# Index tables of a graph kernel: the counts by source come first, VectorE picks places beside the target one-hots, and the sync engine stores the fetched target rows

## The chip, the cores and the metric

The kernel runs on one core of a Trainium2 chip. The metric is the device time of one execution, in microseconds. Each execution runs the whole program: 73632 instructions in the profiled one.

## The reference

The program computes four graph networks one after the other over N = 50000 nodes and E = 25000 edges (`src`, `dst`) with rows of D = 128 floats: a two-layer graph attention, three hops of weighted sums, one round of edge messages, and three layers of a graph convolution, each behind a layer norm with a residual sum. What matters here is the shape that all of them share:

```python
h = gat_conv(x, src, dst, edge_attr, ...)            # gathers rows by src, sums them by dst
msgs = edge_val[:, None] * x[edge_col]               # edge_col = dst: gathers by dst ...
segment_sum(msgs, edge_row, num_segments=n)          # ... sums by edge_row = src
```

So rows are fetched by source and summed by target, or the other way round. The kernel needs for each node the position of its edges in an order by target (the edges come sorted so) and in an order by source, which it makes itself. For that it builds a table `TAB` with two numbers per node, and for each edge a place (`sort_place`) in the first pass of a sort by source. The stage in question makes these two things and copies, beside them, the row `x[dst]` of each edge into a DRAM array `XD`.

## The kernel before, in words

The program is a row of stages, each a block in which all engines take part, and a stage begins when the one before it has ended on every engine. Semaphores order the work inside a stage; nothing in it is placed by a planner.

The 25000 edges lie as 128 partitions by T = 196 columns, and a column is worked on as one tile. Columns go in NB = 14 blocks of U = 14. A node number is split into a low digit (0 to 255, R = 256) and a high digit; one-hot rows of 256 elements for the two digits, multiplied by TensorE, count nodes into a 256 by 256 histogram in PSUM.

`phase_tables` (L533) is the stage that changes. Its engines do this:

- VectorE makes the one-hots of the **source** digits, two instructions a column (L597, L598), into a ring of two blocks. Before block k it waits until TensorE has used block k - 2 (`s_freed`).
- ScalarE makes the one-hots of the **target** digits: two instructions a column (L652, L653) and, at the end of a block, two wide ones (L658) over the whole block. Its ring has two blocks too, and `d_freed` frees them.
- TensorE takes block k of the source (3 matmuls a column, 42 in all, L668 and L669), then block k of the target (2 a column, 28 in all, L675), then block k + 1 of the source, and so on in strict turn. After the last block it signals `counted`.
- VectorE then copies the four count tiles, scans them, has TensorE add over partitions (L682, L685 to L687), forms the table (L622 to L635), signals `tabled`, forms `weights`, and runs `pick_places` (L520): 196 instructions, one a column, of growing length 256 to 451, L525.
- The sync engine waits for `tabled` and writes `TAB`.
- GpSimd runs `fetch_target_rows` (L498): 14 gathers of 128 rows a block into a ring of two blocks (`xd_ring`, L511), and after block k it waits for the gathers of block k - 1 and stores them to `XD` (L504, 896 KB). Before block k it waits for the store of block k - 2, and, by `beside` (L489), for `d_freed` to reach k - 2.

The next stage, `phase_front`, reads `TAB` by 392 gathers on GpSimd from its first instruction on (L473). A later stage, `phase_high_digit` (L693), runs the same `pick_places` while GpSimd gathers.

## Time and profile before

| what | us |
|---|---|
| runs shown, median | 6715.88 |
| runs shown, lowest and highest | 6671.08, 6734.13 |
| profiled execution, first to last instruction | 6034.3 |
| median less this span | 681.6 |
| stage of the tables, POOL's first row to the next stage's first | 141.57 to 508.29 |

The page has no time of the profiled execution itself, only its span; what lies around the span is known as the difference of 681.6 us to the median. The table's last line gives the start of the first index instruction of the stage and of the first DMA issue of the next one. Busy shares of the whole span say little about this stage, which is one of a dozen: VectorE is busy 68% of the span, GpSimd 62%, TensorE 55%, ScalarE 48%. The page's chain of work that ended last is empty here (0% on each engine), so what ends a wait is read from the waits and the timeline of the stage.

### The profile page before, as it was taken

How to read it: one execution, taken by the hardware profiler on the slowest of the kernel's cores; microseconds unless marked ns; L12 is line 12 of the kernel's file. 1: busy time of each engine (PE TensorE's matmuls, PEld its weight loads, DVE VectorE, ACT ScalarE, POOL GpSimd, SP SyncE). 2: the span in 40 equal slices, each digit the busy share in tenths (PEclk: the TensorE clock that was granted, in tenths of full speed). 3: DMA queues.
4: the chain of work that ended last, by engine and by line, in shares of the span. 5: the costliest groups of instructions: out<-in, count | busy, mean ns of one | idle time of the engine just before them, and what ended most of it. 6: DMA issues, size and time to landing. Idle time of an engine off the chain costs nothing. (4 is left out here: it accounts for less than half of the span.)

```text
span 6034.3 us, 73632 instructions
## 1 busy us (share of the span) xinstructions
PE 3347.4 (55%) x17186; PEld 2352.5 (39%) x17363; DVE 4133.5 (68%) x14902; ACT 2890.5 (48%) x6936; POOL 3733.6 (62%) x3700
## 2 busy tenths in 40 slices
PE   0534777737330000777777758888688854454443
PEld 0423554627320000444444436666466644343322
DVE  7359999639491995998989967777377755454332
ACT  0954777313100222666666647777477743232110
POOL 0664776767675576645536546665577627676776
PEclk9767999767665555899999989999899976566666
DMA  2223665637321664434435445554244447564333
GB/s 67 80 93 119 199 200 189 191 91 192 84 51 43 163 186 124 121 109 110 116 100 121 110 128 186 189 188 158 84 151 150 141 143 246 175 200 145 119 123 100
DMA packets 512359, 827.25 MB, mean 137 GB/s; under 512 B 108999, under 2 KB 193843, under 8 KB 510796
## 3 DMA queue, kind: packets, MB, share of 16 engines
q1 hardware_dynamic: 396011, 629.55, 32.2%
q0 software_dynamic: 115936, 193.21, 14.3%
q8 instruction: 136, 2.23, 0.2%
q14 instruction: 276, 2.26, 0.1%
HBM read 382.25 MB, written 452.03 MB: 138 GB/s over the span
## 5 line engine op out<-in xcount | busy, mean ns | idle before, releaser
L3074 POOL DMA_INDIRECT gcn_ring<-GT,gcn_index x588 | 586.6, 998 | 199.1 <-issue 170.1
L3175 DVE SCALAR_TENSOR_TENSOR gcn_acc<-gcn_acc,cont,gcn_ring 128x128 f32<-128x128 f32 x588 | 203.6, 346 | 562.5 <-DMA gcn_ring<-GT,gcn_index 561.4
L1602 POOL DMA_INDIRECT light_ring<-C,light_s_u x392 | 390.5, 996 | 285.9 <-DVE light_acc L1645 178.7
L482 POOL DMA_INDIRECT J<-packed,sort_place x392 | 423.7, 1081 | 155.2 <-issue 120.5
L3257 PE MATMUL gcn_psA<-ident,gcn_h 128*128 128x128 f32 x588 | 154.9, 415 | 598.5 <-DVE gcn_h L3178 598.0
L3224 ACT ACTIVATE gcn_hT<-gcn_psA 128x512 f32<-128x512 f32 x147 | 87.8, 597 | 698.0 <-PE gcn_psA L3257 697.5
L3257 PEld LDWEIGHTS gcn_psA<-ident,gcn_h 128*128 128x128 f32 x588 | 100.1, 207 | 636.9 <-DVE gcn_h L3178 636.9
L1447 ACT ACTIVATE tail_h<-tail_x,tail_nmr,tail_std 128x128 f32<-128x128 f32 x784 | 320.8, 484 | 9.2 <-DVE tail_nmr L1377 9.2
L2321 POOL DMA_INDIRECT out<-source_x,source_own_u x196 | 193.7, 988 | 208.8 <-DVE source_x L2407 163.1
L473 POOL DMA_INDIRECT got_s<-TAB,src_u x196 | 202.1, 1031 | 123.7 <-issue 63.0
L1496 PE MATMUL tail_psT<-ident,tail_h 128*128 128x128 f32 x784 | 128.9, 289 | 266.3 <-ACT tail_h L1447 266.3
L1602 POOL DMA_INDIRECT light_ring<-HD,light_r_u x196 | 195.9, 1000 | 118.3 <-DVE light_acc L1645 63.8
L511 POOL DMA_INDIRECT xd_ring<-in_x,dst_u x196 | 191.6, 977 | 105.3 <-issue 55.9
L1496 PEld LDWEIGHTS tail_psT<-ident,tail_h 128*128 128x128 f32 x784 | 92.4, 144 | 397.2 <-ACT tail_h L1447 370.2
L473 POOL DMA_INDIRECT gat_rows<-T,q_u x196 | 200.0, 1020 | 73.1 <-issue 61.7
L473 POOL DMA_INDIRECT got_d<-TAB,dst_u x196 | 205.0, 1046 | 64.3 <-issue 64.3
L2677 POOL DMA_INDIRECT msg_ps<-PS,msg_s_u x196 | 196.9, 1005 | 66.9 <-issue 57.3
L3067 POOL DMA_INDIRECT out<-gcn_x_then_o,own_idx_u x196 | 200.5, 1023 | 59.7 <-issue 59.1
L2672 POOL DMA_INDIRECT msg_x<-XHX,msg_home_u x196 | 198.3, 1012 | 59.7 <-issue 59.1
L473 POOL DMA_INDIRECT gat_rows<-T,src_u x196 | 186.6, 952 | 77.8 <-issue 61.2
L2313 POOL DMA_INDIRECT source_xs<-XHX,source_q_u x196 | 191.8, 978 | 60.4 <-issue 57.2
L1645 DVE SCALAR_TENSOR_TENSOR light_acc<-light_acc,s_cont,light_ring 128x128 f32<-128x128 f32 x585 | 206.0, 352 | 20.8
(637 smaller groups left out, 12801.6 us busy)
## 6 DMA issues: line engine op xcount, KB each, us to landing
T<-front_t SPq DMA_DIRECT2D x196, 272.0 KB, 2.1
C<-light_acc SPq DMA_DIRECT2D x147, 256.0 KB, 2.1
source_c<-C SPq DMA_DIRECT2D x147, 256.0 KB, 4.9
GT<-source_r SPq DMA_DIRECT2D x147, 256.0 KB, 2.1
gcn_own<-GT SPq DMA_DIRECT2D x147, 256.0 KB, 3.5
RC<-gcn_own SPq DMA_DIRECT2D x147, 256.0 KB, 3.6
RG<-gat_rows SPq DMA_DIRECT2D x98, 264.0 KB, 3.9
front_x<-in_x SPq DMA_DIRECT2D x98, 256.0 KB, 3.7
```

Of the source, the lines that this page charges most:

```text
L473: nc.gpsimd.indirect_dma_start(out=out[:, c, :], out_offset=None, in_=table, in_offset=bass.IndirectOffsetOnAxis(ap=index[:, c:c + 1], axi ...
L482: nc.gpsimd.indirect_dma_start(out=table, out_offset=bass.IndirectOffsetOnAxis(ap=index[:, c:c + 1], axis=0), in_=rows[:, c, :], in_offset ...
L1447: last = nc.scalar.activation(out[:, j, :], rows_[:, j, :], func, bias=self.nmr[:, at % self.MV, i, j, :], scale=self.std[:, at % self.MV, ...
L1496: last = nc.tensor.transpose(ps["T"][:, j * P:(j + 1) * P], rows_[:, j, :], net.ident[:, :])
L1602: nc.gpsimd.indirect_dma_start(out=ring[:, n % RING, j, :], out_offset=None, in_=tables[h], in_offset=bass.IndirectOffsetOnAxis(ap=index[: ...
L1645: nc.vector.scalar_tensor_tensor(out=acc[:, n % AR, j, :], in0=before, scalar=s_.cont[:, g * S + j:g * S + j + 1], in1=ring[:, n % RING, j ...
L2672: nc.gpsimd.indirect_dma_start(out=X[:, n % XR, j, :], out_offset=None, in_=net.XHX, in_offset=bass.IndirectOffsetOnAxis(ap=home_u[:, n * ...
L2677: nc.gpsimd.indirect_dma_start(out=PSr[:, n % PR, j, :], out_offset=None, in_=net.PS, in_offset=bass.IndirectOffsetOnAxis(ap=s_u[:, n * S ...
L3067: nc.gpsimd.indirect_dma_start(out=out, out_offset=bass.IndirectOffsetOnAxis(ap=net.own_idx_u[:, m * S + j:m * S + j + 1], axis=0), in_=o[ ...
L3074: nc.gpsimd.indirect_dma_start(out=ring[:, n % RING, j, :], out_offset=None, in_=net.GT[i], in_offset=bass.IndirectOffsetOnAxis(ap=index[: ...
L3175: nc.vector.scalar_tensor_tensor(out=acc[:, n % 2, j, :], in0=before, scalar=net.cont[:, c:c + 1], in1=ring[:, n % RING, j, :], op0=ALU.mu ...
L3257: ins = nc.tensor.transpose(psA[n % 2][:, j * P:(j + 1) * P], h[:, n % 2, j, :], net.ident[:, :])
```

## The change

TensorE's order: of the first twelve blocks of the source, two are taken for each one of the target, then the last two of the source; the sum over partitions for `totals` follows, and the other eight blocks of the target come behind that. VectorE no longer waits for all counts: with the source counts done it forms `weights` and picks the places, and only then takes the target counts and forms the table. The two halves of the table signal `tabled` separately, so the sync engine waits for 2. The stores to `XD` are issued by the sync engine, which also waits for the last of them ahead of its write of `TAB`. The numbers computed are the same.

```diff
--- before.py
+++ after.py
@@ -495,13 +495,18 @@
     return passed
 
 
-def fetch_target_rows(nc, net, pool, table, index, ring, arrived, stored, passed):
+def store_target_rows(net, sp, ring, arrived, stored):
 
     rows = net.XD.rearrange("(p t) d -> p t d", t=T)
-
-    def store(k):
-        pool.wait_ge(arrived[k % 2], 16 * U * (k // 2 + 1))
-        pool.dma_start(rows[:, k * U:(k + 1) * U, :], ring[:, k % 2, :, :]).then_inc(stored[k % 2], 16)
+    for k in range(NB):
+        sp.wait_ge(arrived[k % 2], 16 * U * (k // 2 + 1))
+        sp.dma_start(rows[:, k * U:(k + 1) * U, :], ring[:, k % 2, :, :]).then_inc(stored[k % 2], 16)
+    for half in range(2):
+        sp.wait_ge(stored[half], 16 * (NB // 2))
+
+
+def fetch_target_rows(nc, pool, table, index, ring, arrived, stored, passed):
+
     for k in range(NB):
         if k >= 2:
             pool.wait_ge(stored[k % 2], 16 * (k // 2))
@@ -510,11 +515,6 @@
             passed(c)
             nc.gpsimd.indirect_dma_start(out=ring[:, k % 2, u, :], out_offset=None, in_=table,
                                          in_offset=bass.IndirectOffsetOnAxis(ap=index[:, c:c + 1], axis=0)).then_inc(arrived[k % 2], 16)
-        if k >= 1:
-            store(k - 1)
-    store(NB - 1)
-    for half in range(2):
-        pool.wait_ge(stored[half], 16 * (NB // 2))
 
 
 def pick_places(nc, v, values, weights, out, junk, picked):
@@ -530,7 +530,7 @@
 JUNK = 4
 
 
-def phase_tables(nc, net, packed, place, src_u, dst_u, fetch):
+def phase_tables(nc, net, packed, place, src_u, dst_u, fetch, store_fetched):
 
 
 
@@ -543,13 +543,13 @@
         iota_b = sb("iota_b", [P, R], BF16)
         s_low, s_high, d_low, d_high = (sb(n, [P, 2, U, R], BF16) for n in ("s_low", "s_high", "d_low", "d_high"))
         cnt = sb("cnt", [P, 2, 2, R])
-        run, node, has = sb("run", [P, 2, 2, R]), sb("node", [P, 2, R]), sb("has", [P, 2, R])
+        run, node, has = sb("run", [P, 2, 2, R]), sb("node", [P, 2, R]), sb("has", [P, 2, 2, R])
         node_i, table = sb("node_i", [P, 2, R], I32), sb("table", [P, 2, R, 2], I32)
         base, totals, unit, offset = sb("base", [P, R]), sb("totals", [P, R]), sb("unit", [P, R]), sb("offset", [P, 2, 2])
         ps = [nc.alloc_psum_tensor(f"tab_ps{i}", [P, 512], F32) for i in range(7)]
         step, s_made, s_freed, d_low_made, d_made, d_freed = (sem(n) for n in ("step", "s_made", "s_freed", "abs_made", "d_made", "d_freed"))
-        ready, counted, t_done, named, stored, tabled, picked, indexed = (sem(n) for n in (
-            "ready", "counted", "t_done", "named", "stored", "tabled", "picked", "indexed"))
+        ready, t_done, named, stored, tabled, picked, indexed = (sem(n) for n in (
+            "ready", "t_done", "named", "stored", "tabled", "picked", "indexed"))
         value = {}
         with nc.Block("tables") as block:
             @block.gpsimd
@@ -561,7 +561,8 @@
 
             @block.sync
             def _(sp):
-                sp.wait_ge(tabled, 1)
+                store_fetched(sp)
+                sp.wait_ge(tabled, 2)
                 sp.dma_start(net.TAB.rearrange("(h p l) k -> p h (l k)", h=2, l=R), table[:, :, :, :].rearrange("p h l k -> p h (l k)")).then_inc(stored, 16)
                 sp.wait_ge(stored, 16)
 
@@ -607,17 +608,30 @@
                 v.wait_ge(named, 2)
                 link(nc.vector.tensor_copy(node[:, :, :], node_i[:, :, :]))
 
-                v.wait_ge(counted, 1)
+                v.wait_ge(s_freed, NB)
                 for h in range(2):
-                    nc.vector.tensor_copy(cnt[:, 0, h, :], ps[h][:, 0:R])
+                    last = nc.vector.tensor_copy(cnt[:, 0, h, :], ps[h][:, 0:R])
+                link(last)
+                value["counts"] = steps[0]
+                for h in range(2):
+                    last = nc.vector.tensor_tensor_scan(run[:, 0, h, :], unit[:, :], cnt[:, 0, h, :], 0.0, ALU.mult, ALU.add)
+                link(last)
+                v.wait_ge(t_done, 1)
+                link(nc.vector.tensor_copy(totals[:, :], ps[6][:, 0:R]))
+                link(nc.vector.tensor_tensor_scan(base[:, :], unit[:, :], totals[:, :], 0.0, ALU.mult, ALU.add))
+                link(nc.vector.tensor_tensor(base[:, :], base[:, :], totals[:, :], ALU.subtract))
+                link(nc.vector.tensor_tensor(weights[:, 0:R], ps[4][:, 0:R], base[:, :], ALU.add))
+                pick_places(nc, v, values, weights, spot, junk, picked)
+                nc.vector.tensor_copy(place[:, :], spot[:, :])
+                v.wait_ge(d_freed, NB)
+                for h in range(2):
                     last = nc.vector.tensor_copy(cnt[:, 1, h, :], ps[2 + h][:, 0:R])
                 link(last)
-                value["counts"] = steps[0]
-                for i in range(2):
-                    for h in range(2):
-                        last = nc.vector.tensor_tensor_scan(run[:, i, h, :], unit[:, :], cnt[:, i, h, :], 0.0, ALU.mult, ALU.add)
+                for h in range(2):
+                    last = nc.vector.tensor_tensor_scan(run[:, 1, h, :], unit[:, :], cnt[:, 1, h, :], 0.0, ALU.mult, ALU.add)
                 link(last)
                 value["runs"] = steps[0]
+                link(nc.vector.tensor_scalar(has[:, :, :, :].rearrange("p i h l -> p (i h l)"), cnt[:, :, :, :].rearrange("p i h l -> p (i h l)"), 0.0, None, ALU.is_gt))
                 v.wait_ge(t_done, 2)
                 link(nc.vector.tensor_scalar(offset[:, :, :], ps[5][:, 0:4].rearrange("p (h i) -> p i h", h=2), -1.0, None, ALU.add))
                 for i in range(2):
@@ -625,21 +639,12 @@
                         last = nc.vector.tensor_scalar(run[:, i, h, :], run[:, i, h, :], offset[:, i, h:h + 1], None, ALU.add)
                 link(last)
 
-                link(nc.vector.tensor_scalar(has[:, :, :], cnt[:, 1, :, :], 0.0, None, ALU.is_gt))
+                nc.vector.scalar_tensor_tensor(out=run[:, 0, :, :], in0=run[:, 0, :, :], scalar=-float(EP), in1=has[:, 0, :, :], op0=ALU.add, op1=ALU.mult)
                 link(nc.vector.scalar_tensor_tensor(out=run[:, 1, :, :], in0=run[:, 1, :, :], scalar=float(N), in1=node[:, :, :], op0=ALU.add, op1=ALU.subtract))
-                link(nc.vector.tensor_tensor(run[:, 1, :, :], run[:, 1, :, :], has[:, :, :], ALU.mult))
-                link(nc.vector.tensor_tensor(table[:, :, :, 0], run[:, 1, :, :], node[:, :, :], ALU.add))
-
-                link(nc.vector.tensor_scalar(has[:, :, :], cnt[:, 0, :, :], 0.0, None, ALU.is_gt))
-                link(nc.vector.scalar_tensor_tensor(out=run[:, 0, :, :], in0=run[:, 0, :, :], scalar=-float(EP), in1=has[:, :, :], op0=ALU.add, op1=ALU.mult))
                 nc.vector.tensor_scalar(table[:, :, :, 1], run[:, 0, :, :], float(EP), None, ALU.add).then_inc(tabled, 1)
-                link(nc.vector.tensor_copy(totals[:, :], ps[6][:, 0:R]))
-                link(nc.vector.tensor_tensor_scan(base[:, :], unit[:, :], totals[:, :], 0.0, ALU.mult, ALU.add))
-                link(nc.vector.tensor_tensor(base[:, :], base[:, :], totals[:, :], ALU.subtract))
-                link(nc.vector.tensor_tensor(weights[:, 0:R], ps[4][:, 0:R], base[:, :], ALU.add))
-                pick_places(nc, v, values, weights, spot, junk, picked)
-                v.wait_ge(tabled, 1)
-                link(nc.vector.tensor_copy(place[:, :], spot[:, :]))
+                link(nc.vector.tensor_tensor(run[:, 1, :, :], run[:, 1, :, :], has[:, 1, :, :], ALU.mult))
+                nc.vector.tensor_tensor(table[:, :, :, 0], run[:, 1, :, :], node[:, :, :], ALU.add).then_inc(tabled, 1)
+                v.wait_ge(tabled, 2)
 
             @block.scalar
             def _(act):
@@ -660,7 +665,7 @@
 
             @block.tensor
             def _(pe):
-                for k in range(NB):
+                def by_source(k):
                     pe.wait_ge(s_made, k + 1)
                     for u in range(U):
                         first, last_ = k == 0 and u == 0, k == NB - 1 and u == U - 1
@@ -668,19 +673,24 @@
                             nc.tensor.matmul(ps[h][:, 0:R], s_high[:, k % 2, u, h * P:(h + 1) * P], s_low[:, k % 2, u, :], start=first, stop=last_)
                         last = nc.tensor.matmul(ps[4][:, 0:R], net.above[:, :], s_low[:, k % 2, u, :], start=first, stop=last_)
                     last.then_inc(s_freed, 1)
+
+                def by_target(k):
                     pe.wait_ge(d_made, k + 1)
                     for u in range(U):
                         first, last_ = k == 0 and u == 0, k == NB - 1 and u == U - 1
                         for h in range(2):
                             last = nc.tensor.matmul(ps[2 + h][:, 0:R], d_high[:, k % 2, u, h * P:(h + 1) * P], d_low[:, k % 2, u, :], start=first, stop=last_)
                     last.then_inc(d_freed, 1)
-                pe.wait_ge(s_freed, NB)
-                pe.wait_ge(d_freed, NB)
-                pe.sem_inc(counted, 1)
+                for k in range(NB):
+                    by_source(k)
+                    if k % 2 == 1 and k < NB - 1:
+                        by_target(k // 2)
                 pe.wait_ge(step, value["counts"])
                 for h in range(2):
                     last = nc.tensor.matmul(ps[6][:, 0:R], net.ones[:, :], cnt[:, 0, h, :], start=h == 0, stop=h == 1)
                 last.then_inc(t_done, 1)
+                for k in range(NB // 2 - 1, NB):
+                    by_target(k)
                 pe.wait_ge(step, value["runs"])
                 nc.tensor.matmul(ps[5][:, 0:2], net.upper[:, :], run[:, :, 0, R - 1], start=True, stop=True)
                 nc.tensor.matmul(ps[5][:, 2:4], net.ones[:, :], run[:, :, 0, R - 1], start=True, stop=False)
@@ -1696,7 +1706,8 @@
             xd_ring = sb("xd_ring", [P, 2, U, D])
             xd_arrived, xd_stored = ([sem(f"xd_{n_}{k}") for k in range(2)] for n_ in ("arrived", "stored"))
             phase_tables(nc, net, packed, place, src_u, dst_u,
-                         lambda pool, passed: fetch_target_rows(nc, net, pool, inp["x"], dst_u, xd_ring, xd_arrived, xd_stored, passed))
+                         lambda pool, passed: fetch_target_rows(nc, pool, inp["x"], dst_u, xd_ring, xd_arrived, xd_stored, passed),
+                         lambda sp: store_target_rows(net, sp, xd_ring, xd_arrived, xd_stored))
 
         def look_up(pool, turned):
             each = S
```

How the orders differ, first TensorE at the end of the stage. Before, the last source block (its last column here) is followed by the last 28 target matmuls, and then the sums over partitions:

```order
L668 MATMUL tab_ps<-tab_s_low,tab_s_high 128x256 x2
L669 MATMUL tab_ps<-tab_s_low,above 128x256
L675 MATMUL tab_ps<-tab_d_low,tab_d_high 128x256 x28
L682 MATMUL tab_ps<-tab_cnt,ones 128x256 x2
L685 MATMUL tab_ps<-tab_run,upper 128x2
L686 MATMUL tab_ps<-tab_run,ones 128x2
```

Now, at the same place:

```order
L673 MATMUL tab_ps<-tab_s_low,tab_s_high 128x256 x2
L674 MATMUL tab_ps<-tab_s_low,above 128x256
L690 MATMUL tab_ps<-tab_cnt,ones 128x256 x2
L682 MATMUL tab_ps<-tab_d_low,tab_d_high 128x256 x224
L695 MATMUL tab_ps<-tab_run,upper 128x2
L696 MATMUL tab_ps<-tab_run,ones 128x2
```

Eight target blocks (224 matmuls) have moved behind the last source block and behind the first sum over partitions.

On GpSimd, from the first gather on, the stores stood between the blocks of gathers, and each block waited for a store that GpSimd had issued one instruction earlier:

```order
L511 DMA xd_ring<-in_x,dst_u 128x128 [waits tab_indexed]
L511 DMA xd_ring<-in_x,dst_u 128x128 x27
L504 DMA XD<-xd_ring 128x1792 [waits xd_arrived0]
L511 DMA xd_ring<-in_x,dst_u 128x128 [waits xd_stored0]
L511 DMA xd_ring<-in_x,dst_u 128x128 x13
L504 DMA XD<-xd_ring 128x1792 [waits xd_arrived1]
L511 DMA xd_ring<-in_x,dst_u 128x128 [waits tab_d_freed,xd_stored1]
```

Now GpSimd has the gathers alone, with the same waits ahead of each block:

```order
L516 DMA xd_ring<-in_x,dst_u 128x128 [waits tab_indexed]
L516 DMA xd_ring<-in_x,dst_u 128x128 x27
L516 DMA xd_ring<-in_x,dst_u 128x128 [waits xd_stored0]
L516 DMA xd_ring<-in_x,dst_u 128x128 x13
L516 DMA xd_ring<-in_x,dst_u 128x128 [waits tab_d_freed,xd_stored1]
```

The 14 stores (L503 now) stand on the sync engine's queue, ahead of the one write of `TAB`, which also waits for the last two of them.

## Rows read from the trace of the kernel before

**Rows 1.** The page's first line.

```profile
span 6034.3 us, 73632 instructions
```

**Rows 2.** Windows: whole table stage; busy us and instructions by engine, clock, DMA share.

```profile
141.40:508.20 366.80, 144.19 (x990) 112.83 (x990) 196.73 (x831) 244.13 (x420) 200.42 (x212) 0.71 0.23 72
```

**Rows 3.** Groups by line, window 141 to 508: busy us, mean ns, idle before.

```profile
L511 POOL DMA_INDIRECT xd_ring<-in_x,dst_u x196 | 191.6, 977 | 105.3 <-issue 55.9 <-DMA XD<-xd_ring 49.3
L525 DVE SCALAR_TENSOR_TENSOR tab_junk<-tab_values,tab_weights 128x256 f32<-128x256 f32 (+48 forms) x196 | 99.6, 577 | 0.0
...
L597 DVE TENSOR_SCALAR tab_s_low<-tab_iota_b,tab_values 128x256 bf16<-128x256 bf16 x196 | 58.6, 300 | 127.0 <-PE tab_ps L669 127.0
...
L504 POOL DMA_DIRECT2D XD<-xd_ring x14 | 8.2, 583 | 1.3 <-DMA xd_ring<-in_x,dst_u 1.3
```

**Rows 4.** Waits, window 141 to 508: total us, times, longest.

```profile
DVE tab_cnt L612 <- PEq L679: 39.7, 1, 39.7
```

**Rows 5.** Timeline, first blocks: start, us, engine, line.

```profile
142.45 1.12 POOL L511 DMA_INDIRECT xd_ring<-in_x,dst_u  x1 [0.18 <-issue]
...
144.01 0.51 ACT L652 ACTIVATE tab_d_low<-tab_iota_b,tab_minus_low 128x256 bf16<-128x256 bf16 x1 [8.76 <-DVE tab_iota_b L583]
...
151.88 0.61 PE L668 MATMUL tab_ps<-tab_s_low,tab_s_high 128*128 128x256 bf16 x2 [12.24 <-DVE tab_s_high L598]
...
161.64 3.23 PE L675 MATMUL tab_ps<-tab_d_low,tab_d_high 128*128 128x256 bf16 x28 [2.11 <-ACT tab_d_high L658]
```

**Rows 6.** Timeline, GpSimd around the first store.

```profile
177.84 0.62 POOL L504 DMA_DIRECT2D XD<-xd_ring  x1
182.06 0.98 POOL L511 DMA_INDIRECT xd_ring<-in_x,dst_u  x1 [3.60 <-DMA XD<-xd_ring]
```

**Rows 7.** Timeline, one target and one source block on PE.

```profile
336.26 6.09 PE L675 MATMUL tab_ps<-tab_d_low,tab_d_high 128*128 128x256 bf16 x28 [8.26 <-ACT tab_d_high L658]
...
342.19 0.38 PE L668 MATMUL tab_ps<-tab_s_low,tab_s_high 128*128 128x256 bf16 x2
...
346.67 0.27 PE L669 MATMUL tab_ps<-tab_s_low,above 128*128 128x256 bf16 x1
```

**Rows 8.** Timeline, end of the counts to the end of the stage.

```profile
388.65 5.51 PE L675 MATMUL tab_ps<-tab_d_low,tab_d_high 128*128 128x256 bf16 x28 [7.17 <-ACT tab_d_high L658]
...
394.31 0.42 DVE L612 COPY tab_cnt<-tab_ps 128x256 f32<-128x256 f32 x1 [39.66 <-PEq L679]
...
404.97 0.40 SPq L565 DMA_DIRECT2D TAB<-tab_table  x1
...
406.95 0.48 DVE L525 SCALAR_TENSOR_TENSOR tab_junk<-tab_values,tab_weights 128x256 f32<-128x256 f32 x1
```

**Rows 9.** Timeline, last GpSimd store, last VectorE row, next stage's first DMA issue.

```profile
447.97 0.57 POOL L504 DMA_DIRECT2D XD<-xd_ring  x1 [1.27 <-DMA xd_ring<-in_x,dst_u]
...
506.64 0.26 DVE L642 CAST sort_place<-tab_spot 128x196 uint32<-128x196 f32 x1
508.29 3.98 SPq L1141 DMA_DIRECT2D front_x<-in_x  x8
```

**Rows 10.** Windows of PE's clock (eighth number), a block at each level.

```profile
178.00:182.00 4.00, 2.89 (x14) 2.08 (x15) 0.00 (x0) 4.00 (x9) 0.46 (x1) 0.50 0.63 246
...
186.00:190.00 4.00, 3.85 (x36) 3.20 (x33) 0.11 (x1) 4.00 (x11) 3.09 (x4) 1.00 0.21 51
```

**Rows 11.** Windows, later stage, POOL alone: gathers beside the same picks.

```profile
1713.00:1813.00 100.00, 78.96 (x69) 0.51 0.22 48
```

**Rows 12.** VectorE picks there: ns min/median/max, first and last start.

```profile
L525 DVE SCALAR_TENSOR_TENSOR high_junk<-high_values,high_weights x196: 482/593/725, 1713.1 to 1812.6; 128x256 f32<-128x256 f32 x1, 128x257 f32<-128x257 f32 x1, 128x258 f32<-128x258 f32 x1, 128x259 f32<-128x259 f32 x1
```

**Rows 13.** DMA issues: size each, median us to landing.

```profile
gat_of_owner<-XD SPq DMA_DIRECT2D x12, 256.0 KB, 4.6
...
xd_ring<-in_x,dst_u POOLq DMA_INDIRECT x196, 2.6
...
TAB<-tab_table SPq DMA_DIRECT2D x1, 512.0 KB, 3.3
```

## The prediction, made before the changed kernel had run

> **What bounds the kernel now.** I read the page's head first: a span of 6034.3 us [rows 1], 681.6 us below the median of the runs, 6715.88 us. The page names no last chain, so the bound of the stage has to be read from its own windows, groups, waits and timeline. The next stage starts only when every engine is done with this one, so a microsecond off this stage's last end is a microsecond off the span.
>
> The window of the stage shows 366.8 us in which no engine is busy throughout: ScalarE 244.1, GpSimd 200.4, VectorE 196.7, TensorE 144.2 [rows 2]. So the stage is a chain over several engines. The groups say how VectorE spends it: it waits 127.0 us for TensorE between blocks of source one-hots, and its 196 picks take 99.6 us [rows 3]; the waits add 39.7 us ahead of the first copy of the counts [rows 4]. The timeline gives the chain. ScalarE starts on the target one-hots at 144.01 and TensorE can use its first block at 161.64 [rows 5] and its fourteenth at 388.65 [rows 8]; that is (388.65 - 161.64) / 13 = 17.46 us a block. TensorE is done 5.5 us after that, VectorE copies counts from 394.31, the write of the table goes out at 404.97, the picks start at 406.95 [rows 8] and the last VectorE row ends at 506.64 + 0.26 = 506.90. The next stage's first DMA issue is at 508.29, 1.4 us later; GpSimd's last store was issued at 447.97 [rows 9]. So the end is **ScalarE's 14 blocks, the table, then the picks**. During the picks ScalarE and TensorE do nothing.
>
> **The order on TensorE.** A target block took 6.09 us for 28 matmuls when TensorE came to it after a wait of 8.26 us, 0.217 us each, and the source block behind it ran from 342.19 to 346.94, 4.75 us for 42, 0.113 each [rows 7]. The clock granted was 0.50 (1.2 GHz) in the one and 1.00 (2.4 GHz) in the other [rows 10]; the first target block, reached after 2.11 us of idle time, took 3.23 us [rows 5]. With two source blocks to each target one, TensorE's work per ScalarE block is 6.09 + 2 x 4.75 = 15.6 us, under 17.46: ScalarE keeps its pace. VectorE needs 2 x 58.6 / 14 = 8.4 us at most for a source block's one-hots [rows 3] (the high digit's instruction at the price of the low one's), 16.8 us for two, so it keeps up as well.
>
> **The source counts.** Six target blocks are in front of the last two source blocks. The sixth can start at 161.64 + 5 x 17.46 = 248.9, ends by 255.0, and two source blocks end at 264.5. Two count copies, the sum over partitions and four short VectorE instructions come next. The same kinds took 406.95 - 394.31 = 12.6 us with the whole table formed between them [rows 8]; the table's share is 404.97 - 394.31 = 10.7 us less the copies, so I take 4.5 us. Nothing shows this mix by itself; it lies between 2 (the difference) and 12.6. **The picks run from 269 to 369** at 99.6 us [rows 3]. The value picked matters little: they have until 394.2, when the target counts are complete, so this work is hidden with 25 us to spare. If that cover went (counts of the source 25 us late), each further microsecond would be paid. The same picks beside GpSimd's gathers took from 1713.1 to 1812.6, 99.5 us [rows 12], so gathers don't slow them. No row has picks beside ScalarE's one-hots; from below and above I take no effect, and at most the 25 us of slack.
>
> **The table.** It still starts at 394.3. Two copies and two scans fewer, one compare fewer, against three instructions that may now follow each other without a wait: at most 10.7 us as before, at least half; I take 7.8, to 402.1. Its write lands 3.3 us after issue [rows 13]: 405.5 by this route. Before, those 3.3 us were hidden under the picks; now they lie on the path.
>
> **The fetch.** Before, GpSimd waited 49.3 us in 12 blocks for stores that it had issued one instruction earlier, and spent 8.2 us issuing them [rows 3]; 4.22 us each from issue to the next gather [rows 6]. None of this was on the path, since GpSimd was done 59 us ahead. Now it would be: 404 us is earlier than 448. On the sync engine a store is issued about 2.6 us [rows 13] after the last gather of its block, while GpSimd gathers the next block; that takes 14 x 1.264 = 17.7 us, the rate being (177.84 - 142.45) / 28 [rows 5, 6]. A store has then 15.1 us to land before GpSimd asks for it. It took 4.2 us from GpSimd's queue; the sync queue moved 256 KB in up to 4.6 us [rows 13], which grown by the bytes would be 16.1 us for 896 KB. So the wait is 0, and by the upper bound 1.0 us in each of 12 blocks. I take 0. GpSimd's wait for target counts is never last: block k may start when target block k - 3 is used, 161.6 + 17.46 (k - 3) + 6.1, against 142.5 + 17.7 k, which is 27 us later.
>
> Beside the picks the gathers get slower: 69 of them began in 100 us [rows 11], against 79 at 1.264 us. The picks now cover 100 us of gathers instead of 41, at a price of 10 x 1.264 = 12.8 us. The last gather starts at 142.45 + 195 x 1.264 + 12.8 = 401.7, lands at 404.3, its store at 408.5, and behind it stands the write of the table, which the sync engine may issue only now: 411.8. **So the sync engine's tail ends the stage, at 411.8**, 6 us behind the VectorE route, and the next stage begins at 413.2.
>
> **The sum.** 508.3 - 413.2 = 95.1 us, from a span of 6034.3. The page gives no time of the profiled execution, only the span; 95 us off the median of 6715.88 gives 6621. If the 681.6 us around the span should mean that a run without the profiler is slower all over, in the ratio 1.113, it would be 106. I take 6620.
>
> **Rivals.**
>
> *TensorE becomes the bound* (0.05). If the clock stayed at 1.2 GHz, 112 matmuls at 0.217 are 24.4 us a pair, 6.9 more than ScalarE's pace. Six pairs and what follows put the sixth target block at 298, and ScalarE's ninth block waits for the seventh: 42 us late in all. The stage would end at 447 and the time be 6656. For it: the clock falls in each wait. Against: it was back at 1.00 by 186, 7 us after TensorE's first matmul of the block at 179, and more work means less idle time.
>
> *The gathers are blocked by the picks* (0.05). If each gather beside the picks waited a whole pick more, 0.577 us [rows 3], only 54 would fit into 100 us, 31.6 us lost in place of 12.8: 6640. Against: 69 began [rows 11]. The Trainium skill, "SBUF — State Buffer", section "Who interferes with whom", says that a VectorE instruction with two SBUF inputs contends with a GpSimd instruction that reads SBUF, and that the loser is fully blocked, not throttled; that would be this rival. The trace agrees that there is contention and has it at 100 / 69 - 1.264 = 0.19 us a gather, a third of a pick.
>
> *The store waits stay* (0.05). If only the issue of the stores left GpSimd and its waits of 49.3 us stayed, the last gather would start at 451, the next stage at 462.5, and the gain be 46: 6670. The Trainium skill, "DMA: Bandwidth & Descriptors", section "Issuing engines are not separate DMA queues", says that issuing from several engines saves only the sequencer's time, which speaks against this half of the change. But the rows put these waits down to the place of the store in GpSimd's program, one instruction ahead of the wait.
>
> *Given back later* (0.05). The next stages start on colder or fuller queues and lose over 28 us: 6660 or so. I find no row for it.
>
> *Slower* (0.03). Place: GpSimd's wait for `xd_stored`. Each microsecond of a store's landing beyond 15.1 is paid 12 times, and to lose 67 us on top of the 95 it has to be 28.6 us: 12 x 13.5 = 162. Time 6783. The largest landing by rows is 16.1, so this needs the sync engine's stores to starve among the gathers.
>
> **The numbers.** My forecast holds 0.77. About 1% (67 us) is what a measurement can tell from no change here; the three runs spread by 63 us. From 95 us, noise takes the forecast into that band once in fourteen, and the first four rivals lie on both sides of it. That gives faster 0.77, within 1% 0.20, slower 0.03. Range: below, 106 us and the lowest run's 45 under the median, 6565; above, the store-wait rival plus some of the spread, 6680.
>
> **What would show it.** Right: picks from about 269, over by 370; the last target block on TensorE still from 388.6; no GpSimd wait on `XD` stores; the last gather at about 402, the write of the table within 12 us of it, the next stage's first issue near 413; 69 to 72 gathers beside the picks. Wrong: ScalarE's blocks over 17.5 us apart, gathers idle at the start of a block, or later stages longer than before.

## The result, and the profile after

| kernel | median us | lowest to highest | runs |
|---|---|---|---|
| before | 6729.04 | 6671.08 to 6773.53 | 12 |
| changed | 6661.51 | 6640.89 to 6704.81 | 12 |

The ratio is 0.9928 [0.9902 to 0.9954]: 48 us (0.0072 x 6729.04) less, with a range of 31 to 66, half of the 95 us forecast. The two medians of the table lie further apart, 67.5 us, just outside that range; this too is less than 95. The median of the changed kernel lies 41.5 us above the forecast and inside its range, but the ratio is within 1% of no change, which had a chance of 0.20.

One thing has to be known to read the numbers: the same program comes out in two kinds of execution, and all runs of one group (kernels timed together on one chip) are of one kind. In some groups the kernel before takes 6036 to 6066 us, in others 6671 to 6946 us; below they are called the quick and the slow kind. Chip number 7 showed both, if the number stands for one chip. The profile read ahead of the prediction is of the quick kind (span 6034.3 [rows 1]), and all 24 runs above are of the slow one.

The changed kernel's profile here is of the slow kind. These are its page's first line (before: 6034.3 us and 73632 instructions [rows 1]) and its DMA, the same 827.25 MB as in the kernel before:

```profile
span 6669.9 us, 73806 instructions
...
DMA packets 512359, 827.25 MB, mean 124 GB/s; under 512 B 108999, under 2 KB 193843, under 8 KB 510796
```

The time of this execution was 6671.72 us, so 1.8 us lie around the span. The 681.6 us that I took to lie around it do not exist.

Groups by line, from 141 to 488 us (busy us, mean ns, then the idle time before them and what ended it), for [rows 3]:

```profile
L516 POOL DMA_INDIRECT xd_ring<-in_x,dst_u x196 | 197.8, 1009 | 122.9 <-issue 59.1 <-PE tab_ps L682 55.8 <-remote 7.9
L525 DVE SCALAR_TENSOR_TENSOR tab_junk<-tab_values,tab_weights 128x256 f32<-128x256 f32 (+48 forms) x196 | 100.9, 583 | 9.6 <-DVE tab_junk L525 6.1 <-issue 3.3
L657 ACT ACTIVATE tab_d_low<-tab_iota_b,tab_minus_low 128x256 bf16<-128x256 bf16 x196 | 96.7, 493 | 73.0 <-PE tab_ps L682 58.4 <-DVE tab_iota_b L584 8.8 <-remote 5.0
```

GpSimd no longer waits for its stores. But it waits 55.8 us for TensorE's target blocks, and so does ScalarE, 58.4 us; neither did before. ("remote" is a wait whose releaser the profile does not name.) The end of the stage in the timeline (start, duration), for [rows 8, 9]:

```profile
464.13 0.33 SPq L503 DMA_DIRECT2D XD<-xd_ring  x1
...
476.04 0.76 DVE L628 COPY tab_cnt<-tab_ps 128x256 f32<-128x256 f32 x2 [3.82 <-PE tab_ps L682]
482.86 0.69 DVE L646 TENSOR_TENSOR tab_table<-tab_run,tab_node 128x512 int32<-128x512 f32 x1
483.66 0.38 SPq L566 DMA_DIRECT2D TAB<-tab_table  x1
487.76 1.29 SPq L1151 DMA_DIRECT2D front_x<-in_x  x3
```

The next stage starts at 487.8 us, where I had 413.2, because the target counts are complete at 476 instead of 394. TensorE's timeline early in the stage shows why:

```profile
165.92 0.63 PE L673 MATMUL tab_ps<-tab_s_low,tab_s_high 128*128 128x256 bf16 x2
168.11 0.37 PE L674 MATMUL tab_ps<-tab_s_low,above 128*128 128x256 bf16 x1 [1.56 <-issue]
170.21 0.37 PE L673 MATMUL tab_ps<-tab_s_low,tab_s_high 128*128 128x256 bf16 x1 [1.73 <-issue]
173.01 0.37 PE L673 MATMUL tab_ps<-tab_s_low,tab_s_high 128*128 128x256 bf16 x1 [2.43 <-issue]
175.81 0.37 PE L674 MATMUL tab_ps<-tab_s_low,above 128*128 128x256 bf16 x1 [2.43 <-issue]
...
197.51 0.37 PE L673 MATMUL tab_ps<-tab_s_low,tab_s_high 128*128 128x256 bf16 x1 [2.43 <-issue]
```

Each matmul takes 0.37 us, and between two of them stand 1.6 to 2.4 us in which TensorE waits for nothing that the profile shows. Such stretches come again, shorter, near 217 to 228, 244 to 255, 269 to 281, 296 to 306 and 320 to 331. No stretch of this kind stands on TensorE in this stage in a trace of the quick kind.

### The profile page after: what moved, and what is told of

Same layout as the page of the kernel before. It is cut to its first block and busy times, and to the rows that moved or that the text cites. A ratio compares the mean times of both kernels' runs of the same rounds, so it can differ in the third digit from the quotient of the medians.

```text
span 6669.9 us, 73806 instructions
## 1 busy us (share of the span) xinstructions
PE 3505.5 (53%) x17363; PEld 2458.0 (37%) x17363; DVE 4180.8 (63%) x14901; ACT 2893.8 (43%) x6936; POOL 3715.1 (56%) x3686
## 2 busy tenths in 40 slices
DMA packets 512359, 827.25 MB, mean 124 GB/s; under 512 B 108999, under 2 KB 193843, under 8 KB 510796
## 5 line engine op out<-in xcount | busy, mean ns | idle before, releaser
L3268 PE MATMUL gcn_psA<-ident,gcn_h 128*128 128x128 f32 x588 | 132.0, 365 | 478.4 <-DVE gcn_h L3189 269.0
L947 PE MATMUL gcn_psB<-w_conv,gcn_hT 128*128 128x128 f32 x784 | 144.4, 344 | 251.4 <-ACT gcn_hT L3235 146.7
L3228 ACT ACTIVATE gcn_o<-gcn_psB,dinv 128x128 f32<-128x128 f32 x392 | 112.2, 371 | 283.9 <-DMA GT<-gcn_o 116.3
```

The costliest lines, as they stand in the source:

```text
L3268: ins = nc.tensor.transpose(psA[n % 2][:, j * P:(j + 1) * P], h[:, n % 2, j, :], net.ident[:, :])
```

## The experiments

In the table below "stage end" is the next stage's first DMA issue (508.29 in [rows 9]), read in each trace. Kernels of one group ran on one chip. "One profile" is a single further execution of the kernel before; the time beside the group's number is the median of all its runs of the kernel before.

| group, kind | kernel | ratio to before, 95% interval | stage end us |
|---|---|---|---|
| 1, quick, 6048.7 us | before (one profile) | | 507.52 |
| | stores by sync alone | 1.0003 [0.9993, 1.0012] | 507.23 |
| | order alone | 0.9910 [0.9896, 0.9925] | 456.83 |
| | change | 0.9842 [0.9827, 0.9856] | 412.80 |
| 2, slow, 6869.1 us | before (one profile) | | 557.18 |
| | change + matmuls | 1.0036 [1.0005, 1.0067] | 572.53 |
| | before + matmuls | 1.0140 [1.0084, 1.0195] | 624.21 |
| | three to two | 0.9972 [0.9936, 1.0008] | 526.79 |
| 3, slow, 6718.0 us | change | 0.9946 [0.9902, 0.9991] | 485.25 |
| | order alone | 0.9958 [0.9921, 0.9996] | 487.82 |
| | change + matmuls | 1.0071 [1.0029, 1.0113] | 552.70 |
| | late settle | 0.9918 [0.9884, 0.9953] | 484.79 |
| 4, quick, 6054.5 us | before (one profile) | | 507.64 |
| | change | 0.9837 [0.9812, 0.9862] | 412.77 |
| | stores by sync alone | 0.9994 [0.9982, 1.0006] | 507.62 |
| | late settle | 0.9840 [0.9821, 0.9859] | 411.42 |
| 5, slow, 6889.0 us | before (one profile) | | 554.37 |
| | change + matmuls | 1.0022 [0.9968, 1.0076] | 558.19 |

Groups 3 and 4 ran under the same chip number, 7.

### Group 1: the two halves, and the change once more

The first kernel is the one before, unedited. "Stores by sync alone" is the kernel before with this of the change, and "order alone" is the change with this taken back:

```diff
+def store_target_rows(net, sp, ring, arrived, stored):
...
+        sp.wait_ge(arrived[k % 2], 16 * U * (k // 2 + 1))
+        sp.dma_start(rows[:, k * U:(k + 1) * U, :], ring[:, k % 2, :, :]).then_inc(stored[k % 2], 16)
...
-        if k >= 1:
-            store(k - 1)
-    store(NB - 1)
...
+                store_fetched(sp)
```

> The kernel before, unchanged, for a second profile. The profile of before had a span of 6034 us while its timed runs lay between 6671 and 6774 us, and the profile of the changed kernel has 6670 us. Theory A (that first profile is of an untypical execution; in typical ones engines also lose time to slow issue, as the changed kernel's profile shows on TensorE, ScalarE and VectorE, where one instruction in 1.4 to 2.8 us is issued in stretches): the new span is 6670 to 6770 us, the table stage ends at 520 to 545 us in place of 508, and such stretches show in it. Theory B (the execution was typical, the changed kernel brought the slow stretches): the new span is near 6034 us and its table stage ends at 508 us without such stretches.

> The kernel before with one half of the change: the sync engine issues the stores of the fetched rows; the orders on TensorE and VectorE are as before. Theory A (GpSimd was not on the path while the picks ended the stage): ratio 0.997 to 1.003, and GpSimd's last gather is over 45 to 55 us earlier than before. Rival C (the stores on the sync engine's queue delay the refills of the engines' instructions or other transfers): slower by 10 to 30 us. Rival D (the measured 48 us come from this half): faster by 30 us or more.

> The changed kernel with the stores back on GpSimd: the new order on TensorE and VectorE alone. By my sum GpSimd then ends the stage: its last gather near 451 us, the next stage's first issue near 460 us, against 413 for the whole change, in an execution without slow stretches. Theory A: about half of the gain of the whole change is left, ratio 0.995 to 0.999. Rival C (the sync engine's stores cost something that this kernel saves): as fast as the whole change or faster, ratio 0.993 or less. Rival E (what limits the changed stage is instruction issue on TensorE and ScalarE, not GpSimd): the same 0.993 as the whole change, and the stage ends within 5 us of the changed kernel's.

> The changed kernel, unchanged, on the same chip as the others: ratio 0.990 to 0.996 as measured already, with a second profile. Theory A (the slow stretches come at the same instructions in every typical execution): TensorE again issues one matmul in 2 to 3 us for some 30 us in the second source block, near 165 to 201 us, and the stage ends near 486 us. Rival F (they fall by chance): the stretches lie at other places and the stage's end differs by over 10 us.

The kernel before took 6039.02 us with a span of 6037.3: again nothing lies around the span. The expectations above have two theories. What A said of this profile and of the changed kernel (spans of 6670 us and more, slow stretches, a ratio of 0.990 to 0.996) did not come, nor did B's slow stretches brought by the change: the whole group was of the quick kind, so it settles what happens there and says nothing of the slow kind. The order alone was to have a ratio of 0.995 to 0.999 and had 0.9910.

The change gained 95.4 us (6048.7 to 5953.3), **the 95 us of the forecast**, and in the stage 507.52 - 412.80 = 94.7. Its timeline from the end of the source counts to the next stage:

```profile
261.04 0.75 DVE L613 COPY tab_cnt<-tab_ps 128x256 f32<-128x256 f32 x2 [6.14 <-PE tab_ps L674]
...
393.99 0.75 DVE L628 COPY tab_cnt<-tab_ps 128x256 f32<-128x256 f32 x2 [28.17 <-PE tab_ps L682]
...
400.93 0.75 DVE L646 TENSOR_TENSOR tab_table<-tab_run,tab_node 128x512 int32<-128x512 f32 x1
...
402.21 0.94 POOL L516 DMA_INDIRECT xd_ring<-in_x,dst_u  x1 [0.30 <-issue]
404.64 0.33 SPq L503 DMA_DIRECT2D XD<-xd_ring  x1
408.69 0.38 SPq L566 DMA_DIRECT2D TAB<-tab_table  x1
412.80 1.29 SPq L1151 DMA_DIRECT2D front_x<-in_x  x3
```

Forecast and row: source counts 264.5 and 261.0; target counts 394.2 and 394.0, behind a wait of 28.17 us that was to be 25; table done 402.1 and 401.7; last gather 401.7 and 402.2; table write 408.5 and 408.7; next stage 413.2 and 412.8.

The halves: the stores by the sync engine alone give nothing, since the picks end the stage. The order alone gives 50.7 us in the stage, because GpSimd is then last: its last store is issued at 448.4, and the stage ends at 456.83 (near 460 was expected). Its groups there, for [rows 3]:

```profile
L511 POOL DMA_INDIRECT xd_ring<-in_x,dst_u x196 | 196.8, 1004 | 100.7 <-issue 55.9 <-DMA XD<-xd_ring 44.7
```

Those 44.7 us are what moving the stores takes away: 456.83 - 412.80 = 44.0 us. A part that is worth 0 alone is worth 44 us beside the other.

### Group 2: more work for TensorE, and another order

The further profile of the kernel before has no edit. "+ matmuls" adds to either kernel, behind each source column's own three matmuls:

```diff
+                        for _ in range(3):
+                            nc.tensor.matmul(ps[5][:, R:2 * R], net.above[:, :], s_low[:, k % 2, u, :], start=True, stop=True)
```

"Three to two" changes the order and, as a second edit, where the sync engine waits for its last stores:

```diff
-                    if k % 2 == 1 and k < NB - 1:
-                        by_target(k // 2)
+                    if k % 3 and k < NB - 2:
+                        by_target(taken)
+                        taken += 1
...
                 sp.wait_ge(stored, 16)
+                settled(sp)     # the wait for the last XD stores, until now ahead of the table write
```

> The kernel before, unchanged, for a profile of it. On a chip like the one of the forecast the span is 6034 to 6060 us, no engine has stretches of one instruction per 2 us, and the stage ends at 507 to 509 us. On a chip like the one of the official comparison (6671 to 6773 us) the slow issue theory expects such stretches on TensorE between 160 and 330 us here too, and, because the stage before pairs its one-hots otherwise and ends on picks that run after the counts, an end of the stage at 530 to 550 us: 45 to 60 us behind the 487.8 us of the changed kernel there. The rival, that only work after this stage is slower there, expects an end near 508 us and so a gain of 20 us in the stage.

> The changed kernel with three more matmuls behind each source column's own three, of the same stationary and moving operands, into a half of a PSUM bank that nobody reads (42 more for a source block, 588 in all): TensorE's work for a source block is doubled, nothing else is touched. Theory (in the changed order one target and two source blocks share TensorE within one 17.46 us of ScalarE, so it has less than 2 us to spare, and a slower TensorE stretches the counting): the pair becomes 6.1 + 2 x 9.5 = 25 us at the mean matmul of before, 22 where the extra ones run at their streaming time; ScalarE waits for TensorE in each block while source blocks last (seven pairs), the source counts are done 30 to 50 us later, and the stage ends 25 to 45 us after the 412.8 us of the changed kernel; ratio to the kernel before 0.989 to 0.993 where the change alone had 0.984. Rival (TensorE has room, or the picks cover it): the stage ends within 5 us of 412.8 and the ratio stays 0.984 to 0.985.

> The kernel before with the same three extra matmuls behind each source column's own. Theory: there one source block goes with one target block within 17.46 us of ScalarE, 6.1 + 9.5 = 15.6 us of TensorE, so nothing waits longer: the stage ends at 507 to 510 us and the ratio is 0.999 to 1.001. Rival (any slowing of TensorE costs either order the same): the stage ends 25 to 45 us later and the ratio is 1.004 to 1.007, so that the change would keep its whole gain on a chip where TensorE is slower.

> The changed kernel with the source blocks spread wider (after every source block but each third a target block is counted, 8 target blocks before the source blocks end instead of 6), and with the sync engine waiting for the last XD stores to land only after it has issued the table write. TensorE has 6.1 + 1.5 x 4.75 = 13.2 us of work per 17.46 us. Theory: where engines issue at full pace the picks start some 35 us later (near 300 us) and take 100 us, so they end at 400 to 405 instead of 366, VectorE comes to the target picks at 405 to 410 instead of 394, and the table write is issued at 411 to 416; the later wait for the stores gives back 3 to 4 us; the stage ends at 413 to 418 against 412.8, ratio 0.984 to 0.986. Where engines issue slowly in stretches, ScalarE waits less for TensorE and the stage ends 10 to 30 us sooner than the changed kernel's 487.8. Rival (order has no effect on the end): 409 to 410 us, ratio 0.983 to 0.984.

This group was of the slow kind. The kernel before has the stretches as well, at other places in its order, and its stage ends at 557.18, later than the 530 to 550 that I expected. Its counts are complete at 442.7 against 393.6, 49 us late, and the picks, 99 us, follow. My expectation for the kernel before with more matmuls failed: no cost was forecast (15.6 us of TensorE under 17.46), and it was 67.0 us in the stage (624.21 - 557.18). With the extra matmuls ScalarE waits for TensorE 104.0 us in 12 blocks:

```profile
ACT tab_d_low L652 <- PE tab_ps L677: 104.0, 12, 18.9
```

On the slow kind **TensorE sets the pace in the order of before too**, even without them. On the quick kind TensorE waited for each of ScalarE's 14 blocks:

```profile
PE tab_ps L675 <- ACT tab_d_high L658: 100.1, 14, 9.7
```

On the slow kind the same kernel waits for one of them:

```profile
PE tab_ps L675 <- ACT tab_d_high L658: 4.8, 1, 4.8
```

The account of the quick kind (room in the old order, none in the new) is thus not tested by this pair, since both fell on a slow kind.

"Three to two" was to shorten ScalarE's waits and gain 10 to 30 us. It ended at 526.79. Its source counts are done at 387.4 us, so that the picks run from 392.5 to 514.3 and VectorE reaches the target counts only at 514.5, 34 us after TensorE has finished its last target block:

```profile
475.89 4.64 PE L681 MATMUL tab_ps<-tab_d_low,tab_d_high 128*128 128x256 bf16 x28 [12.63 <-ACT tab_d_high L662]
```

The waits of ScalarE were not the end of that stage; the picks were. The changed kernel itself has no profile in this group; less the 67.5 us that its extra matmuls cost in group 3, it would have ended at 505.0 (an estimate), 22 us sooner than three to two. So more targets early looks like the wrong direction on the slow kind.

### Group 3: change and order alone on a slow kind

Change, order alone and change + matmuls as above; "late settle" is the change with only the second edit of "three to two".

> The changed kernel once more, beside the other three of this call. Two kinds of chip have been seen: one where the kernel before takes 6035 to 6060 us and the changed one ends the stage at 412.8 us against 507.5, and one where it takes 6670 to 6930 us, TensorE has stretches of one instruction per 0.7 to 2.8 us, the kernel before ended the stage at 557.9 us (one such chip) and the changed one at 488.4 (another). First kind: ratio 0.984, stage end 412 to 414. Second kind, theory (the gain in the stage is what remains, 60 to 75 us, and the rest of the program gives nothing back): stage end 480 to 500, and the time 50 to 75 us under the kernel before, ratio 0.989 to 0.993. Rival (part of the stage's gain is lost later there): under 45 us of gain with the stage at 480 to 500.

> The new order of the tables with the stores of target rows left on GpSimd. First kind of chip: 0.991 and a stage end at 457 us, as it was, since GpSimd's 14 waits for landings make its chain the last. Second kind, theory (TensorE's slow stretches put the target counts at 470 to 480 us, behind a GpSimd chain that ended at 435 to 446 even with its store waits): the stage ends within 10 us of the changed kernel on the same chip, so moving the stores gives nothing there and the ratio is within 0.002 of the changed kernel's. Rival (GpSimd's gathers are bound to TensorE's pace by their flow control, and the store waits add to it): the stage ends 25 to 45 us after the changed kernel's.

> The changed kernel with its source matmuls doubled, as before. On the first kind of chip, theory: a pair is 22 to 25 us of TensorE against 17.46 of ScalarE, the stage ends 25 to 45 us after the changed kernel's, ratio 0.989 to 0.993. Rival: within 5 us, 0.984 to 0.985. On the second kind: 70 to 90 us after the changed kernel's on the same chip (on one such chip the stage ended at 573 us), ratio 1.002 to 1.006.

> The changed kernel with one thing moved: the sync engine waits for the last XD stores to land after it has issued the table write instead of ahead of it. First kind of chip: the table is ready at 401.7 us and its write left at 408.7, behind the landing of the last store; now it leaves at 402 to 405 and the stage ends with the last store's landing, at 409 to 410 instead of 413: 3 to 4 us sooner, ratio 0.001 lower at most, which this comparison can hardly tell. Second kind: the last store landed 15 us ahead of the table write, so 0 us. Rival: on the first kind GpSimd's last gather is late and the end does not move.

The stage ends went the way of the theory, the times not all. The changed kernel's stage ended at 485.25 (480 to 500 expected; 487.76 in the profile shown first), but its time was only 36 us [6 to 66] under the kernel before by the ratio, 40 by the medians, where the theory had 50 to 75 and the rival, that part of the gain is lost later, under 45. The extra matmuls were to cost 70 to 90 us in the stage and a ratio of 1.002 to 1.006; they cost 67.5 and the ratio was 1.0071. Order alone ends 2.6 us after the change, so the half that was worth 44 us gives next to nothing here. Waits of GpSimd and ScalarE in order alone, for [rows 3]:

```profile
L511 POOL DMA_INDIRECT xd_ring<-in_x,dst_u x196 | 197.4, 1007 | 129.0 <-issue 56.0 <-PE tab_ps L681 54.6 <-DMA XD<-xd_ring 18.4
L656 ACT ACTIVATE tab_d_low<-tab_iota_b,tab_minus_low 128x256 bf16<-128x256 bf16 x196 | 96.7, 493 | 77.8 <-PE tab_ps L681 68.1 <-DVE tab_iota_b L583 8.8 <-issue 0.9
```

GpSimd waits 54.6 us for TensorE's target blocks, and most of its waits for stores fall into that time: 18.4 us are left of 44.7. The 588 extra matmuls cost the changed kernel 552.70 - 485.25 = 67.5 us, 0.115 each, about what a source matmul takes when TensorE runs without pause (0.113 [rows 7]). So TensorE had no spare time at all while source blocks lasted. (Over the whole run the extra matmuls cost more than in the stage, on either kernel: 84 us by the ratios here, 96 in group 2, where the stage shows 67.0. What follows the stage is thus not the same length in every kernel on the slow kind.)

The two windows before and after 201 us make the contrast (busy us and instructions of PE, PEld, DVE, ACT, POOL, then clock, DMA share and GB/s, as in [rows 2]). The changed kernel, quick kind, group 1:

```profile
142.00:201.00 59.00, 41.69 (x331) 34.82 (x332) 49.00 (x236) 57.32 (x103) 44.96 (x47) 0.92 0.30 99
201.00:347.00 146.00, 75.79 (x571) 60.89 (x568) 122.29 (x515) 145.73 (x256) 112.16 (x106) 0.78 0.28 92
```

The changed kernel, slow kind, group 3:

```profile
142.00:201.00 59.00, 13.77 (x64) 7.26 (x64) 14.90 (x69) 35.29 (x60) 40.12 (x42) 0.68 0.29 94
201.00:347.00 146.00, 97.97 (x692) 73.00 (x692) 70.17 (x345) 100.47 (x179) 75.13 (x79) 0.78 0.20 67
```

The kernel before, slow kind, group 5:

```profile
142.00:201.00 59.00, 19.33 (x87) 9.74 (x88) 21.14 (x97) 35.18 (x60) 41.60 (x44) 0.67 0.22 69
201.00:347.00 146.00, 88.72 (x557) 61.60 (x557) 46.05 (x224) 137.96 (x240) 94.61 (x102) 0.73 0.25 85
```

In the first 59 us TensorE gets through 64 matmuls instead of 331. From 201 on the order of before lets ScalarE work 138.0 of 146 us, the new one 100.5: the new order puts more TensorE work ahead of each target block, and where TensorE is late, ScalarE and GpSimd wait.

### Groups 4 and 5: before and change side by side

> The kernel before, unchanged, for a profile on the same chip as the next three. First kind of chip: stage end 507 to 508 us. Second kind, theory (the changed kernel's lost gain is lost in this stage, where TensorE's slow stretches cost the kernel before some 35 to 50 us and the changed one 75): stage end 530 to 560 us, and the difference to the changed kernel's stage end on this chip is within 20 us of the difference of the medians. Rival (the kernel before loses as much as the changed one, and the gain is given back after the stage): stage end 575 us or more, 90 us or more behind the changed kernel.

> The changed kernel beside it. First kind: stage end 412 to 414 us, ratio 0.984. Second kind: 480 to 500 us and a ratio of 0.990 to 0.995, from 45 to 70 us less in the stage and nothing given back.

> The kernel before with nothing but its stores of target rows moved to the sync engine. Both theories: the picks end the stage on either kind of chip, so it ends where the kernel before ends it (within 3 us) and the ratio is 0.999 to 1.001 on the first kind, 0.997 to 1.003 on the second.

> The changed kernel with the sync engine's wait for the last XD stores behind its table write. First kind: stage end 409 to 410 us against 412.8, 3 to 4 us sooner. Second kind: within 2 us of the changed kernel's stage end (485.4 against 485.9 so far), the ratio anywhere within 0.003 of it.

> The kernel before, for a profile beside the next run. First kind of chip: stage end 507 to 508 us. Second kind: 535 to 560 us, which is 5 to 25 us ahead of the changed kernel with more matmuls (573.2 against 557.9 on the one chip where both were profiled), so that with the 67.5 us that the extra matmuls cost the changed kernel the change's own gain in the stage comes to 45 to 60 us. Rival (the kernel before loses as much as the changed one on such chips): it ends 30 us or more behind the changed kernel with more matmuls.

> The changed kernel with its source matmuls tripled in part (42 more of the same per source block). First kind of chip, theory: one target and two source blocks are then 6.1 + 2 x 9.5 = 25 us of TensorE (22 at streaming pace) against 17.46 of ScalarE; the source counts are done 30 to 50 us later than 261 us, the stage ends 25 to 45 us after 412.8, ratio 0.988 to 0.992 instead of 0.984. Rival (it has room): stage end within 5 us of 412.8, ratio 0.984. Second kind: stage end 553 to 575 us and a ratio of 1.002 to 1.008, as in both runs so far.

Group 4 fell on the quick kind, under the chip number that had been slow in group 3, and repeated group 1: 99.7 us by the medians, 94.9 in the stage, 0 for the stores alone. The late settle was to give 3 to 4 us; it gave 1.35:

```profile
404.55 0.33 SPq L503 DMA_DIRECT2D XD<-xd_ring  x1
405.33 0.38 SPq L564 DMA_DIRECT2D TAB<-tab_table  x1
411.42 2.25 SPq L1150 DMA_DIRECT2D front_x<-in_x  x5
```

The table write leaves 3.3 us sooner, but on the heels of the store, and the next stage then comes 6.1 us behind it instead of 4.1. The times cannot tell it from the change: ratios of 0.9840 and 0.9837.

Group 5 was of the slow kind, and gives the kernel before beside the changed one with more matmuls: 554.37 and 558.19. Less the 67.5 us of the extra matmuls, the change itself would end at 490.7 there, a gain of 63.7 us (45 to 60 had been expected); by the same sum group 2 gives 557.18 - (572.53 - 67.5) = 52.2. So the gain in the stage on the slow kind comes to **52 to 64 us in place of 95**. This is an estimate: the 67.5 us were measured in group 3 alone. Without it, but across groups whose times differ by 140 us and more, the two ends seen of each kernel (554.37 and 557.18, 485.25 and 487.76) lie 67 to 72 us apart. By either way the rival that the kernel before loses as much as the changed one is out: it would have left 95. The slow kind delays the end of before by 47 and 50 us (554.37 and 557.18 against 507.6), and that of the change by 72 and 75 where it was seen (485.25 and 487.76), 78 and 92 by these sums. The gains by the clock of whole runs are 48 [31 to 66], 36 [6 to 66] and, with the late settle, 55 us [32 to 78]. They fit a stage gain of 52 to 64 with nothing given back later, but would also fit 10 us or more given back; that is not settled. What follows the stage took 6145 to 6366 us in the traces of the slow kind (span less stage end), with some 85 us between the kernels of one group, so single profiles can't settle it. Nor is there a profile of before and of the unedited change in one group of the slow kind.

## Why the prediction was wrong

**The steps inside the stage held** on the executions that the forecast was made from: in two groups of the quick kind the gain was 95.4 and 99.7 us, and every time in the list under group 1 is within 3.5 us of its forecast. The 4.5 us taken from the source counts to the picks had the widest bounds of the sum (2 to 12.6) and came out at 4.2 (261.04 to 265.27), which is partly luck. (The price of the gathers beside the picks, 10 x 1.264, is 12.6 and not 12.8, which changes nothing.) The picks beside ScalarE's one-hots, which no row had shown, took 100.2 us against 99.6. With the picks beside them, 70 gathers began in 100 us, where 69 were forecast:

```profile
265.50:365.50 100.00, 77.28 (x70) 0.64 0.27 91
```

That also answers the rival of blocked gathers (54). In the 100 us before, without picks, 80 began. And the rival by which the store waits stay is out: with the stores issued by the sync engine GpSimd has no wait on an `XD` store, in any trace.

**The step that failed** is the use of this in the sum: "95 us off the median of 6715.88", with the 681.6 us taken as lying around the span or as a slower run all over. They lie inside the span. The timed runs were of a kind in which engines issue in slow stretches, and the profile was of the kind in which they don't. My alternative was a gain stretched with the time, 106 us; in fact it shrank. In the prediction's terms it was the overlap that went: "TensorE's work per ScalarE block is 6.09 + 2 x 4.75 = 15.6 us, under 17.46: ScalarE keeps its pace". In the changed kernel of group 3 ScalarE's wide one-hots start at 244, 270, 295, 319 and 346 us, 25.5 us apart, and the target counts, which were to be complete at 394.2, are complete at 473.5 (476.0 in the profile shown first). The prediction's signs of being wrong, ScalarE's blocks over 17.5 us apart and gathers idle at the start of a block, both showed.

**The mechanism is the first rival's**, which had 0.05: TensorE becomes the bound. I priced it with the clock, 24.4 us for the three blocks; the 25.5 us came from the slow issue instead. The rival's time, 6656, is close to the 6661.5 measured, but partly by luck: it had the stage end at 447 instead of 485 to 488, and knew nothing of the 47 to 50 us that the kernel before loses as well.

The chance was misjudged with it. I had 17.46 - 15.6 = 1.9 us of TensorE's time to spare for each ScalarE block, the old order 17.46 - 10.8 = 6.6. A change that trades a waiting engine's slack for order is exposed to anything that slows that engine, and a median 11% above the profiled span said that something did.

## What to carry to other kernels

Compare the span of the profile with the median first. Here a span lies about 2 us under the time of its own execution, and the median lay 11% above the span read first. So far apart, the timed runs may be another kind of execution: ask which engine could be slow in it, and how much slack the new order leaves it. And judge a part of a change beside its other parts: the moved stores gave 0, 44 or 3 us, as the chain beside them ended.

## What the runs showed of the hardware

- The same program on one core took 6036 to 6066 us in some groups of runs and 6671 to 6946 in others, under one chip number both. In the slow kind TensorE issues one matmul per 0.7 to 2.8 us in stretches of up to 42 us (159.3 to 201.0 in group 3); the steps are close to multiples of 0.7 us. The picks on VectorE do it too, from 380 to 397 in that trace. What causes it is open. The traces of before and of the change have 136 transfers of 16 KB on the queue of kind "instruction" (135 or 136 within the span) in either kind, with a median of 0.97 to 1.03 us each in both, so slower transfers alone don't explain it.
- The next stage's first DMA issue comes 4.1 us after the table write's when the store ahead of it has landed (408.69 to 412.80 in group 1), and 6.1 us after it when the write follows a store of 896 KB by 0.8 us (405.33 to 411.42 in group 4). In the second case the sync engine waits 2.8 us for that store and 1.6 us for the write.
- A gather beside picks costs 100 / 70 - 100 / 80 = 0.18 us more on average, in this stage as in the later one ([rows 11]).
